# Attention scores from two float32r parts in 48 rows, instead of three bf16 parts in 96, with each half of the keys in its own half of the rows

## What is computed

```python
q = split_heads(layernorm(x) @ Wq.T + bq); k = split_heads(ctx @ Wk.T + bk); v = split_heads(ctx @ Wv.T + bv)
attn = softmax(einsum('bhqd,bhkd->bhqk', q, k) / sqrt(16))
x = x + tanh(g_xattn) * (merge_heads(attn @ v) @ Wo.T + bo)
z = layernorm(x)                       # then 1 shared and 8 routed experts, top 2 of 8
x = x + tanh(g_ffn) * (shared(z) + sum_e cw_e * expert_e(z))
```

## Time and profile before

| | us |
|---|---|
| runs before | 862.84, 867.04, 868.81; median 867.04 |
| profiled execution, first to last instruction (span) | 864.9 |
| TensorE busy | 807.7 (93%) |
| VectorE busy | 592.1 (68%) |
| ScalarE busy | 475.4 (55%) |
| POOL busy | 131.2 (15%) |

### The profile page before, as it was taken

How to read it: one execution, slowest core, us unless ns; L and a number is a source line. 1 busy time by engine, 2 the same in 40 slices (tenths; PEclk the granted TensorE clock), 3 DMA queues, 4 the chain that set the end, 5 groups by cost and what they waited for, 6 DMA issues and landing times.

```text
span 864.9 us, 12980 instructions
## 1 busy us (share of the span) xinstructions
PE 807.7 (93%) x4040; PEld 456.2 (53%) x4040; DVE 592.1 (68%) x832; ACT 475.4 (55%) x842; POOL 131.2 (15%) x142
## 2 busy tenths in 40 slices
PE   3886868999999999999999899999999999999997
PEld 3774522233333323333333347777877778777885
DVE  6799797688888888888888336956465536554443
ACT  4574346677777777777777863343334333442331
POOL 7433133023000000000000009700000000000000
PEclk9798879899999999999999999999999999999999
DMA  7698959666555455565510004201100110011100
GB/s 256 238 240 319 216 146 150 108 103 114 75 75 75 73 75 85 85 85 85 86 52 7 3 23 151 69 31 40 53 24 25 40 57 24 24 37 61 36 26 24
DMA packets 70530, 75.67 MB, mean 87 GB/s; under 512 B 15801, under 2 KB 51906, under 8 KB 70498
## 3 DMA queue, kind: packets, MB, share of 16 engines
q1 hardware_dynamic: 69202, 68.19, 37.2%
q0 software_dynamic: 1296, 7.08, 2.4%
HBM read 52.96 MB, written 22.09 MB: 87 GB/s over the span
## 4 chain that ended last, share of the span: by engine, by line
PE 76%; DVE 12%; DMA 4%; issue 3%; ACT 3%; SPq 1%; POOL 0%; DVEq 0%; ACTq 0%; POOLq 0%
PE psH L1274 19%; PE psO L1147 13%; PE psS L1120 13%; PE psM L1102 11%; PE psY L1261 10%; DVE mneg L774 2%; DVE tL L768 2%; PE psX L1207 2%; PE psV L1062 1%; DMA qst<-msb 1%; DVE kf L791 1%; PE psF L1076 1%; DVE mneg L845 1%; ACT pr L613 1%; DMA attn<-ast 1%
## 5 line engine op out<-in xcount | busy, mean ns | idle before, releaser
L845 DVE TENSOR_REDUCE mneg<-psM 128x1 f32<-128x1024 f32 x240 | 282.6, 1219 | 66.1 <-PE psM L1102 66.0
L613 ACT ACTIVATE pr<-psS 128x512 f32<-128x512 f32 x488 | 266.7, 595 | 97.1 <-PE psS L1120 96.8
L1120 PE MATMUL psS<-qst,kst 99*128 99x512 bf16 x488 | 153.8, 388 | 7.3 <-DMA qst<-msb 4.7
L1147 PE MATMUL psO<-pr,vt 128*32 128x512 f32 x1024 | 138.1, 612 | 0.1
L1102 PE MATMUL psM<-kst,qst 96*128 96x512 bf16 x480 | 127.6, 386 | 6.4 <-DVE mneg L845 4.2
L1120 PEld LDWEIGHTS psS<-qst,kst 99*128 99x128 bf16 x488 | 40.0, 97 | 156.0 <-ACT pr L613 132.6
L960 DVE TENSOR_TENSOR sil<-sil,cwb 128x512 f32<-128x512 f32 x64 | 47.7, 745 | 91.5 <-ACT sil L680 89.1
L687 ACT CAST gH<-g 128x512 fp32r<-128x512 f32 x72 | 44.7, 621 | 116.9 <-DVE g L964 116.9
L680 ACT ACTIVATE sil<-psH,b_s 128x512 f32<-128x512 f32 x72 | 49.5, 687 | 79.9 <-PE psH L1274 78.4
L1102 PEld LDWEIGHTS psM<-kst,qst 96*128 96x128 bf16 x480 | 46.3, 98 | 65.8 <-DVE mneg L845 10.8
L964 DVE SCALAR_TENSOR_TENSOR g<-psH,b_s,sil 128x512 f32<-128x512 f32 x72 | 54.1, 751 | 37.2 <-ACT sil L680 35.0
(11 more groups left out here) (145 smaller groups left out, 1047.7 us busy)
## 6 DMA issues: line engine op xcount, KB each, us to landing
kst<-k_parts SPq DMA_DIRECT2D x96, 128.0 KB, 5.1
v_pad<-vst SPq DMA_DIRECT2D x16, 512.0 KB, 7.5
vt<-v_pad SPq DMA_DIRECT2D x16, 512.0 KB, 7.3
cwb<-cw_rows SPq DMA_DIRECT2D x32, 256.0 KB, 3.3
wraw<-wexp POOLq DMA_DIRECT2D x9, 768.0 KB, 4.6
k_parts<-parts SPq DMA_DIRECT2D x16, 384.0 KB, 5.7
qst<-q_parts SPq DMA_DIRECT2D x96, 64.0 KB, 4.6
ctxt<-ctx SPq DMA_DIRECT2D x8, 512.0 KB, 6.8
```

The source lines that it names most:

```text
L613: nc.scalar.activation(pr[:, slot, j], score_bank(s, j), ACT.Exp, scale=SCALE).then_inc(e_done, 1)
L845: V.tensor_reduce(mneg[:, parity, i:i + 1], psM[:, i % 2], X_AXIS, ALU.max, negate=True).then_inc(m_free, 1)
L1120: mm(score_bank(s, j), kst[:, slot, j, kt * P:(kt + 1) * P], qst[:, slot, j], start=True, stop=True).then_inc(s_full, 1)
L1147: last = mm(psO[j * VW:(j + 1) * VW, u % 2], vt[:, u, k, j * VW:(j + 1) * VW], pr[:, k % 4, j], start=(k == 0), stop=(k == KT - 1), skip_g ...
```

## The change

- Two float32r parts replace the three bf16 parts. `TERMS` has three products (high x high, high x low, low x high), so a score needs 3 x 16 = 48 rows, with the maximum's rows (two now) 50.
- `kst` and `qst` hold two groups of rows, from 0 and from 64. The first half of the keys lies in the first group, the second half in the second, and the queries in both. The two matmuls of a maximum tile use one group each. In a score step the blocks of keys alternate between the halves from head to head (`key_tile`), so neighbouring score matmuls use different groups.
- `kf`, POOL's third part, VectorE's cast and the second of ScalarE's copies are gone; VectorE makes the low part in one operation from PSUM.
- `split_max` has two links instead of four; four DMAs bring the maximum's rows instead of three.
- In bytes the parts in DRAM grow from 3 x 2 to 2 x 4 per element, and the queries of a unit are loaded twice. The number of load DMAs per unit stays 12.
- `EARLY` falls from 3 to 1, and `wA_raw` now shares the place of `wraw`.

```diff
--- before.py
+++ after.py
@@ -41,14 +41,16 @@
...
 UNITS = NB * NG
-TERMS = ((0, 0), (0, 1), (1, 0), (1, 1), (0, 2), (2, 0))
+TERMS = ((0, 0), (0, 1), (1, 0))
 SROWS = len(TERMS) * DH
-MROWS = SROWS + 3
+MROWS = SROWS + 2
+GROUP = 64
+HK = NK // 2
 VW = 32
...
 FF = 256
-EARLY = 3
+EARLY = 1
 WCOLS = DT * 2 * FF + DT * D
@@ -57,8 +59,8 @@
...
-    q_parts = dram("q_parts", [NB, 3, D, NQ], BF16)
-    k_parts = dram("k_parts", [NB, 3, D, NK], BF16)
+    q_parts = dram("q_parts", [NB, 2, D, NQ], F32)
+    k_parts = dram("k_parts", [NB, 2, D, NK], F32)
...
@@ -124,10 +127,10 @@
...
-        msb = sb("msb", [HG * QT, 2, 3, P], BF16, sB)
+        msb = sb("msb", [HG * QT, 2, 2, P], F32R, sB)
...
-        kst = sb("kst", [MROWS, NG, HG, NK], BF16, sB)
-        qst = sb("qst", [MROWS, NG, HG, NQ], BF16, sB)
+        kst = sb("kst", [P, NG, HG, HK], F32R, sB)
+        qst = sb("qst", [P, NG, HG, NQ], F32R, sB)
...
@@ -289,20 +292,21 @@
...
 
-                        sp.wait_ge(k_ok, 2 + 6 * b + 2 * c + m + 1)
+                        sp.wait_ge(f_taken, 2 + 6 * b + 2 * c + m + 1)
                         dst = q_parts[b] if c == 2 else k_parts[b, :, :, c * BLK:(c + 1) * BLK]
                         sp.dma_start(dst[:, m * P:(m + 1) * P, :].rearrange("s p t -> p s t"),
-                                     parts[:, c, m]).then_inc(qk_st[c], 16)
+                                     parts[:, c, m].bitcast(F32)).then_inc(qk_st[c], 16)
 
...
 
-                for t, (qp, kp) in enumerate(TERMS):
-                    rows = slice(t * DH, (t + 1) * DH)
-                    heads = slice(u * HG * DH, (u + 1) * HG * DH)
-                    sp.dma_start(qst[rows, u], q_parts[b, qp, heads, :].rearrange("(h d) t -> d h t", d=DH)
-                                 ).then_inc(unit_ld[u], 16)
-                    sp.dma_start(kst[rows, u], k_parts[b, kp, heads, :].rearrange("(h d) t -> d h t", d=DH)
-                                 ).then_inc(unit_ld[u], 16)
+                heads = slice(u * HG * DH, (u + 1) * HG * DH)
+                for half in range(2):
+                    for t, (qp, kp) in enumerate(TERMS):
+                        rows = slice(half * GROUP + t * DH, half * GROUP + (t + 1) * DH)
+                        sp.dma_start(qst[rows, u].bitcast(F32), q_parts[b, qp, heads, :].rearrange("(h d) t -> d h t", d=DH)
+                                     ).then_inc(unit_ld[u], 16)
+                        sp.dma_start(kst[rows, u].bitcast(F32), k_parts[b, kp, heads, half * HK:(half + 1) * HK].rearrange(
+                            "(h d) t -> d h t", d=DH)).then_inc(unit_ld[u], 16)
 
@@ -310,13 +314,16 @@
...
 
-                for s in range(3):
-                    sp.dma_start(qst[SROWS + s:SROWS + s + 1, u], msb[:, u % 2, s, :]).then_inc(m_ld[u], 16)
+                for half in range(2):
+                    for s in range(2):
+                        row = half * GROUP + SROWS + s
+                        sp.dma_start(qst[row:row + 1, u].bitcast(F32), msb[:, u % 2, s, :].bitcast(F32)).then_inc(m_ld[u], 16)
 
...
                     sp.wait_ge(qk_st[c], 32 + 32)
+                sp.wait_ge(ones_k, 2)
                 load_unit(0, 0)
...
@@ -441,36 +448,22 @@
...
 
-            nc.gpsimd.memset(kst[SROWS:MROWS], 1.0).then_inc(ones_k, 1)
-            pool.wait_ge(ones_k, 1)
+            for half in range(2):
+                nc.gpsimd.memset(kst[half * GROUP + 32:(half + 1) * GROUP].bitcast(F32), 1.0).then_inc(ones_k, 1)
+            pool.wait_ge(ones_k, 2)
 
...
                 nc.gpsimd.tensor_tensor(msb[:, parity, 0], mcp[:], none[:].to_broadcast([HG * QT, P]), ALU.subtract).then_inc(m_chain, 1)
-                pool.wait_ge(m_chain, 3 * n + 1)
-                nc.gpsimd.tensor_tensor(mcp[:], mcp[:], msb[:, parity, 0], ALU.subtract).then_inc(m_chain, 1)
-                pool.wait_ge(m_chain, 3 * n + 2)
-                nc.gpsimd.tensor_tensor(msb[:, parity, 1], mcp[:], none[:].to_broadcast([HG * QT, P]), ALU.subtract).then_inc(m_chain, 1)
-                pool.wait_ge(m_chain, 3 * n + 3)
-                nc.gpsimd.tensor_tensor(msb[:, parity, 2], mcp[:], msb[:, parity, 1], ALU.subtract
+                pool.wait_ge(m_chain, n + 1)
+                nc.gpsimd.tensor_tensor(msb[:, parity, 1], mcp[:], msb[:, parity, 0].bitcast(F32), ALU.subtract
                                         ).then_inc(mt_split, 1)
-
-            def third_parts(b):
-                for c in range(3):
-                    for m in range(DT):
-
-                        pool.wait_ge(r_ok, 6 * b + 2 * c + m + 1)
-                        nc.gpsimd.tensor_tensor(parts[:, c, m, 2], kf[:, m], parts[:, c, m, 1],
-                                                ALU.subtract).then_inc(k_ok, 1)
-
 
...
             nc.gpsimd.dma_start(wraw[:, 1], wexp[1]).then_inc(raw_ld[1], 16)
-            with pool.Fori(0, NB) as b:
-                third_parts(b)
             split_max(0, 0)
@@ -555,13 +548,9 @@
...
 
-                    act.wait_ge(k_ok, i + 1)
-
                     act.wait_ge(qk_st[c], 32 * (b + 1))
-                    bias = bq_s[:, 0 if c == 2 else 1, m:m + 1]
-                    nc.scalar.activation(kf[:, m], psF[:, m], ACT.Identity, bias=bias)
                     nc.scalar.activation(parts[:, c, m, 0], psF[:, m], ACT.Identity,
-                                         bias=bias).then_inc(f_taken, 1)
+                                         bias=bq_s[:, 0 if c == 2 else 1, m:m + 1]).then_inc(f_hi, 1)
 
@@ -781,15 +770,17 @@
...
 
-            def second_parts(b, c, base):
+            def low_parts(b, c):
                 if c != 1:
...
 
-                    dve.wait_ge(f_taken, 2 + 6 * b + 2 * c + m + 1)
-                    chain(V.tensor_tensor(kf[:, m], kf[:, m], parts[:, c, m, 0], ALU.subtract), base + m + 1)
-                    V.tensor_copy(parts[:, c, m, 1], kf[:, m]).then_inc(r_ok, 1)
+                    dve.wait_ge(f_hi, 6 * b + 2 * c + m + 1)
+                    V.scalar_tensor_tensor(out=parts[:, c, m, 1], in0=psF[:, m],
+                                           scalar=bq_s[:, 0 if c == 2 else 1, m:m + 1],
+                                           in1=parts[:, c, m, 0].bitcast(F32), op0=ALU.add,
+                                           op1=ALU.subtract).then_inc(f_taken, 1)
 
...
@@ -1043,9 +1035,9 @@
...
-                        last = mm(psE[:, half * BLK:(half + 1) * BLK],
-                                  qst[0:SROWS, 0, h, qt * P:(qt + 1) * P],
-                                  kst[0:SROWS, 0, h, half * BLK:(half + 1) * BLK], start=True, stop=True)
+                        rows = slice(half * GROUP, half * GROUP + SROWS)
+                        last = mm(psE[:, half * BLK:(half + 1) * BLK], qst[rows, 0, h, qt * P:(qt + 1) * P],
+                                  kst[rows, 0, h], start=True, stop=True)
@@ -1099,12 +1091,15 @@
...
                 for half in range(2):
-                    last = mm(psM[:, i % 2, half * BLK:(half + 1) * BLK],
-                              qst[0:SROWS, slot, h, qt * P:(qt + 1) * P],
-                              kst[0:SROWS, slot, h, half * BLK:(half + 1) * BLK], start=True, stop=True)
+                    rows = slice(half * GROUP, half * GROUP + SROWS)
+                    last = mm(psM[:, i % 2, half * BLK:(half + 1) * BLK], qst[rows, slot, h, qt * P:(qt + 1) * P],
+                              kst[rows, slot, h], start=True, stop=True)
                 last.then_inc(m_full, 1)
 
-            def score_tile(s, slot, kt, j):
+            def key_tile(k, j):
+                return k // 2, (k + j) % 2
+
+            def score_tile(s, slot, k, j):
 
@@ -1117,19 +1112,21 @@
...
                     pe.wait_ge(e_done, 4 * s + j + 1)
-                mm(score_bank(s, j), kst[:, slot, j, kt * P:(kt + 1) * P], qst[:, slot, j], start=True,
+                kt, half = key_tile(k, j)
+                rows = slice(half * GROUP, half * GROUP + MROWS)
+                mm(score_bank(s, j), kst[rows, slot, j, kt * P:(kt + 1) * P], qst[rows, slot, j], start=True,
                    stop=True).then_inc(s_full, 1)
...
             pe.wait_ge(v_taken, 2 + 4 * NB)
-            pe.wait_ge(ones_k, 1)
+            pe.wait_ge(ones_k, 2)
             pe.wait_ge(unit_ld[1], 16 * 12)
...
                 if i == BEFORE:
-                    pe.wait_ge(m_ld[0], 48)
+                    pe.wait_ge(m_ld[0], 64)
                 if i >= BEFORE:
@@ -1144,7 +1141,9 @@
...
                 for j in range(HG):
-                    last = mm(psO[j * VW:(j + 1) * VW, u % 2], vt[:, u, k, j * VW:(j + 1) * VW], pr[:, k % 4, j],
+                    kt, half = key_tile(k, j)
+                    last = mm(psO[j * VW:(j + 1) * VW, u % 2], vt[:, u, half * KT // 2 + kt, j * VW:(j + 1) * VW],
+                              pr[:, k % 4, j],
                               start=(k == 0), stop=(k == KT - 1), skip_group_check=True)
@@ -1157,7 +1156,7 @@
...
 
```

(2 more changed lines are left out.)

33 lines of the change are left out of this document (17 added, 16 removed).

## The result

The changed kernel takes 903.17 us (median of 4 runs, 898.32 to 912.18) beside 865.48 for the kernel before on the same chip: ratio 1.043, 95% interval 1.038 to 1.048. One of the four, 912.18, ran in a slower state of the chip; ratios here compare the fast executions only, medians are over all. The direction and the cost of a step were as forecast, the whole was not: 887 with a range to 898. The profiled execution took 901.5 us, its span is 899.7 (before: 864.9).

A forecast was written before the change was run, and what follows sets the result against it. Bound: a 2.89 us chain through values, scores and exponentials per attention step. Steps +21, unit 0's wait +3, projections -7, EARLY +3 gave +20 us, 885 on the span, about 887 us; range 874 to 898, with rivals 861 to 898.

The forecast's parts named there:

- the loop: Attention step: values, third score, two exponentials, next step's second score, next values; these links fill the whole 2.89 us.
- Two exposed loads of 0.11 us: Attention step: float32r weight loads of the third and second scores can't hide, +0.11 us each, giving 3.10 us.
- The rival of hidden loads: Attention: loads hide behind the other half's streaming, step stays 2.884, 862 us; one load or none exposed: chance 0.18.
- the gain of TensorE as the bound: Rival in attention: the step falls to VectorE's 2.46 us, -47 us, total 819 us; chance 0.07.
- about 1 us lower: Attention weight loads: what the forecast sum would be if a load took the skill's 107 ns.
- Unit ends: Last step of an attention unit: 3.19 us with halves side by side, 3.38 one after the other; taken 3.28.
- The projections: Projection stage before attention: less VectorE work, partly offset by TensorE and DMA; -7 us (-13 to +2).
- Unit 0: First attention unit: larger unit loads lengthen TensorE's wait for the first row maxima, +3 us (0 to +5).
- later unit loads have room: Attention after unit 0: a load with its values takes 17 us, maxima behind it needed some 19 us into a unit.
- Units 13 to 15: Last attention units: longer steps only, a +2.5 us share of the predicted terms.
- EARLY: Experts 1 and 2 prepared after attention: TensorE waits 3.7 us, POOL works longer beside VectorE; +3 us (+1 to +7).
- The clock: Rival in attention: TensorE's clock falls in a tenth of the steps, +13 us, total 900 us; chance 0.05.

The follow-up runs named there:

- e5: Changed kernel with exponentials over 256 of the 512 columns, the rest filled with ones once: 872.52 us, ratio 1.010.
- e6: Kernel before with exponentials over half the columns, the rest filled with ones once: 856.78 us, ratio 0.992.
- e10: Changed kernel with the fourth score put in the idle bank of the values' sums in six steps of a unit: 872.01 us, ratio 1.008.
- e1: Kernel before with the same bytes of the score operands read as float32r instead of bf16: 886.97 us, ratio 1.026.
- e14: Changed kernel with the scores reading the upper halves of the same float32r numbers as bf16: 877.32 us, ratio 1.017.
- e2: Kernel before with EARLY = 1 and nothing else: 875.09 us, ratio 1.011.

## Why the prediction came out as it did

- **The bound, and the loop: right.** Each link was read from one step, and e5, e6 and e10 confirm that the loop, and not TensorE's 313.8 busy us of 314.5, is the limit.
- **Two exposed loads of 0.11 us: right.** 3.09 measured for 3.10, and 23 us by e1 and by e14. The rival of hidden loads is out, and the gain of TensorE as the bound too; a gain would have needed the third bank of e10. One recorded figure beside it is wrong: by a load of 107 ns the sum would not be "about 1 us lower" but nearly 19 (83 ns at two places in 112 steps), close to the rival of hidden loads; the 190 ns of the earlier trace rows decided rightly.
- **Unit ends: halves do run side by side** (3.19). I had taken the middle, 3.28; units 1 to 11 came to +14.4 for +16.5.
- **The projections: -7 was too small.** This pair of profiles gives -12.0. The start of the value matmuls scatters from run to run: 120.1 on average in the eleven profiles with the changed projections (118.4 to 122.6), 129.5 in the seven with those before (127.6 to 131.4), so -9.3. VectorE's new operation took 746 ns for the 751 assumed.
- **Unit 0: +3 for the wait and 1 for steps, measured +7.2.** The wait itself grew less than forecast, from 4.7 to 6.1 us. What was left out is the clock: 4.1 us in the three steps before the wait (4.55, 4.55, 4.25 us), which the wait has nothing to do with, and some 1.3 in the two behind it (4.55 and 4.40 for 4.34 and 3.27 before).
- **Unit 12: missed.** The step that failed is "later unit loads have room". The 17 us it gives to a unit load with its values came true (issued at 427.84, landed at 444.76), and the store behind it landed at 445.14. But I compared the load with the next need of its data, and not with SyncE, which in the last batch waits for that store and then has the maxima queued behind the router's loads: 6.5 us more than the steps explain.
- **Units 13 to 15: +2.5, measured +4.5.** Three steps are long: 3.58 in unit 13, behind unit 12's slow steps, and 5.21 and 4.90 in unit 15 for 4.06 and 3.57 before; the granted clock of the stretch is 0.92 instead of 0.97.
- **EARLY: +3 was the worst term**, and the largest part of the miss; it measured 9.4 us in e2 (3 to 16 by its interval) and 12.8 in the profiles. The wait at expert 1 was right (3.7), and the wait of 1.76 us for VectorE did go. The step that failed is the price of POOL working beside VectorE "for some 13 us longer": I looked at how much longer the first batch is, and not at which of VectorE's operations would fall beside POOL. It was the normalisation, with TensorE waiting for what stands behind it, 5.9 us; another wait for VectorE is 2.55 for 2.15. The waits over 1 us of the stretch so add up to 12.1 us instead of 3.9, and the rest of the 12.8 fits the lower granted clock of the first batch, 0.94 for 0.98. The slow normalisation stood nowhere in my sum, though the trace before had one line of VectorE's (`gL`, L969) at 2.06 us beside POOL and at 0.68 without.
- **The clock.** My rival let it fall in steady steps, where it stayed at 1.00. It fell behind each long wait instead, and ahead of unit 0 among the first row maxima, and I charged neither.

What was missed on the slow side, 3 (unit 0), 6.5 (unit 12), 2 (units 13 to 15) and 10 (EARLY), less 5 (projections) and 2 (units 1 to 11) on the fast side, is 14.5 of the 14.8 us between +20 and +34.8.
